# Scan stage of a hybrid kernel: skip term on TensorE, normalising on ScalarE, end-decay product on GpSimd

## What is computed

```python
xn = (x - mean) * rsqrt(var + 1e-5) * ln_w + ln_b          # over channels
z, xBC, dt = split(in_proj_w @ xn)                         # 256, 256 + 32 + 32, 8 rows
xBC = silu(depthwise_conv_3x3(xBC) + conv_b)               # xs (8 heads x 32), B, C
dt = softplus(dt + dt_bias);  A = -exp(A_log)
# chunks of 128 positions, 8 an image
Acs = cumsum(dt * A)                                        # within the chunk
Y_diag = sum_s C_q.B_s * exp(Acs_q - Acs_s) * (xs*dt)_s     # s <= q, by head
state  = sum_q B_q * exp(Acs_end - Acs_q) * (xs*dt)_q       # end decay
Y_off  = C_q . previous_state * exp(Acs_q)
y = Y_diag + Y_off + D * xs                                 # skip term D*xs
y = y * silu(z);  y = y * rsqrt(mean(y*y) + 1e-5) * rms_w
x = x + out_proj_w @ y
```

## Time and profile before

| what | value |
|---|---|
| median of 3 runs | 2489.66 us (2485.59 to 2492.06) |
| profiled execution, its own time | 2490.13 us |
| span of the profile | 2488.4 us, 41622 instructions |
| PE busy | 2235.4 us (90%) |
| DVE busy | 1699.6 us (68%) |
| ACT busy | 1279.2 us (51%) |
| POOL busy | 1635.1 us (66%) |
| mean granted TensorE clock | 0.914 |

### The profile page before, as it was taken

One profiled execution on the slowest core, in us unless ns is written; L12 is line 12 of the kernel. 1 busy time (PEld: TensorE's weight loads), 2 busy tenths in 40 slices (PEclk: granted clock), 3 DMA queues, 4 the chain that ended last, 5 costly groups with the idle time before them and its releaser, 6 DMA issues. The chain is left out here.

```text
span 2488.4 us, 41622 instructions
## 1 busy us (share of the span) xinstructions
PE 2235.4 (90%) x12035; PEld 1803.0 (72%) x12035; DVE 1699.6 (68%) x4560; ACT 1279.2 (51%) x2815; POOL 1635.1 (66%) x1774
## 2 busy tenths in 40 slices
PE   4798898899886999999999999999999997499994
PEld 2466666666664888888888888888888886388883
DVE  5787987888745667767767777677777775244444
ACT  3454554554532666666666666666666664133331
POOL 2688878887861666576685776766757766355551
PEclk9887887787876999999999999999999998699996
DMA  2930000000000001010010010100100100355555
GB/s 89 387 128 9 9 9 1 9 1 1 18 5 23 1 2 24 2 30 13 7 36 1 12 31 4 37 4 8 35 2 12 31 4 30 129 194 189 197 180 203
DMA packets 135413, 131.05 MB, mean 53 GB/s; under 512 B 82885, under 2 KB 101359, under 8 KB 135190
## 3 DMA queue, kind: packets, MB, share of 16 engines
q1 hardware_dynamic: 124950, 107.12, 14.1%
q0 software_dynamic: 9088, 17.07, 2.0%
q10 hardware_dynamic: 1152, 4.19, 0.4%
HBM read 64.78 MB, written 65.10 MB: 52 GB/s over the span
## 5 line engine op out<-in xcount | busy, mean ns | idle before, releaser
L1191 POOL TENSOR_TENSOR plo<-pf,phi 128x512 fp32r<-128x512 f32 (+3 forms) x768 | 775.3, 1018 | 414.5 <-ACT phi L1414 385.3
L1412 ACT ACTIVATE pf<-psum 128x512 f32<-128x512 f32 (+3 forms) x768 | 379.3, 494 | 479.1 <-PE psum L1252 339.1
L1414 ACT ACTIVATE phi<-psum 128x512 fp32r<-128x512 f32 (+3 forms) x768 | 377.1, 491 | 0.0
L1301 PE MATMUL psum<-xT,qT 128*128 128x512 f32 (+3 forms) x768 | 286.1, 372 | 43.9 <-DVE nmax L1557 30.2
L1557 DVE CUSTOM_DVE_ANT_0 masked<-psum,ahead_wide 128x128 f32<-128x128 f32 (+3 forms) x512 | 248.2, 485 | 66.9 <-PE psum L1301 60.2
L1250 PE MATMUL psum<-phi,x_tok 128*128 128x512 f32 (+3 forms) x768 | 289.0, 376 | 0.8 <-POOL plo L1191 0.8
L1252 PE MATMUL psum<-qT,xT 128*128 128x512 f32 (+3 forms) x768 | 266.5, 347 | 0.0
L1251 PE MATMUL psum<-qT,xT 128*128 128x512 f32 (+3 forms) x768 | 266.1, 347 | 0.0
L1250 PE MATMUL psum<-qT,xT 128*128 128x512 f32 (+3 forms) x768 | 265.7, 346 | 0.0
L1251 PE MATMUL psum<-plo,x_tok 128*128 128x512 f32 (+3 forms) x768 | 265.0, 345 | 0.0
L1252 PE MATMUL psum<-phi,x_tok 128*128 128x512 f32 (+3 forms) x768 | 265.0, 345 | 0.0
(11 more groups left out here) (288 smaller groups left out, 5324.5 us busy)
## 6 DMA issues: line engine op xcount, KB each, us to landing
wg<-turned_w SPq DMA_DIRECT2D x39, 874.0 KB
routed<-empty SPq DMA_DIRECT2D x1, 34056.0 KB, 95.7
xg<-routed SPq DMA_DIRECT2D x39, 264.0 KB
qT<-nmax SPq DMA_DIRECT2D x512, 0.5 KB
y<-chosen SPq DMA_DIRECT2D x8, 1024.0 KB, 10.3
turned_w<-wT SPq DMA_DIRECT2D x8, 874.0 KB
x_in_sb<-in_x SPq DMA_DIRECT2D x8, 512.0 KB, 3.3
out<-o_st ACTq DMA_DIRECT2D x8, 512.0 KB, 5.2
```

The lines of the kernel that those rows point to most:

```text
L1191: g_.tensor_tensor(plo[:, T % RP, 0:n], pf[:, T % RP, 0:n], phi[:, T % RP, 0:n].bitcast(F32), ALU.subtract).then_inc(a["low_ready"], 1)
L1301: t.matmul(bank[3][:, 0:n], qT[:, g % 2, 0, i * P:(i + 1) * P], xT[:, b % 2, 0, k0:k0 + n], start=True, stop=True).then_inc(a["peak_ready" ...
L1412: s_.activation(pf[:, T % RP, 0:n], bank[T % RS][:, 0:n], ACT.Exp)
L1414: s_.activation(phi[:, T % RP, 0:n], bank[T % RS][:, 0:n], ACT.Exp).then_inc(a["high_ready"], 1)
```

## The change

Three operations of the scan change engines, and one becomes part of another.

1. The skip term: `dx` and its add on GpSimd go. At the setup VectorE makes `skip_w`, two 128x128 matrices with D on the diagonal. In TensorE's `chunk_y`, ahead of each four heads, xs of the chunk times `skip_w` starts the sum in the half bank, and the heads add to it.
2. The normalising goes from VectorE to ScalarE: `rstd * x + shift`, with `shift` = -mean * rstd made by GpSimd in `deviation` in two more small operations. ScalarE does all eight at j = 6, behind the exponentials and ahead of the first `turned_back`.
3. `Xd` goes from VectorE to GpSimd, a step later, in a new function `chunk_end`; VectorE copies the last column of Ldec (128x8) to `to_end` for it, and waits for `tok_ready` instead of `tok_copied` and `xdt_ready`.

Waits that stood on `tok_ready` for xs no longer being read now stand on `y_ready`, since TensorE reads xs a step later.

```diff
 GpSimd, deviation(n)
                         g_.tensor_tensor(rstd[:, :], mvx[:, :, 1], epst[:, 0:1].to_broadcast([P, NC]), ALU.add).then_inc(s["vx_ready"], 1)
-                        pool.wait_ge(s["vx_ready"], n + 1)
+                        g_.tensor_tensor(shift[:, :], mvx[:, :, 0], minus[:, 0:1].to_broadcast([P, NC]), ALU.mult).then_inc(s["vx_ready"], 1)
+                        pool.wait_ge(s["vx_ready"], 2 * (n + 1))
                         g_.tensor_tensor(rstd[:, :], rstd[:, :], mhalf[:, 0:1].to_broadcast([P, NC]), ALU.pow
                                          ).then_inc(s["rstd_ready"], 1)
+                        pool.wait_ge(s["rstd_ready"], n + 1)
+                        g_.tensor_tensor(shift[:, :], shift[:, :], rstd[:, :], ALU.mult).then_inc(s["shift_ready"], 1)
 GpSimd, silu_x(n, m)
-                        need(pool, "tok_ready", (n - 1) * NC)
+                        need(pool, "y_ready", (n - 1) * NC)
 GpSimd, end of chunk_in(g), and a new function
-                        need(pool, "yd_ready", g - 3)
-                        g_.tensor_tensor(dx[:, g % 4, :].rearrange("p (h d) -> p h d", d=HD), xs3,
-                                         dvec[:, :].unsqueeze(2).to_broadcast([P, NH, HD]), ALU.mult).then_inc(s["dx_ready"], 1)
+                    def chunk_end(g):
+                        pool.wait_ge(s["to_end_ready"], g + 1)
+                        pool.wait_ge(s["xdt_ready"], g + 1)
+                        need(pool, "st_ready", g - 1)
+                        g_.tensor_tensor(Xd[:, g % 2, :].rearrange("p (h d) -> p h d", d=HD),
+                                         xdt[:, g % 2, :].rearrange("p (h d) -> p h d", d=HD),
+                                         to_end[:, g % 4, :].unsqueeze(2).to_broadcast([P, NH, HD]), ALU.mult).then_inc(s["xd_ready"], 1)
 GpSimd, chunk_gate(g)
-                        pool.wait_ge(s["dx_ready"], g + 1)
-                        g_.tensor_tensor(y1[:, g % 4, :], y1[:, g % 4, :], dx[:, g % 4, :], ALU.add).then_inc(s["yd_ready"], 1)
-                        pool.wait_ge(s["yd_ready"], g + 1)
 GpSimd, the loop, between chunk_rs(step - 3) and chunk_in(step)
+                        if 0 <= step - 1 < G:
+                            chunk_end(step - 1)
 TensorE, chunk_y(g)
                         for h in range(NH):
+                            if h % 4 == 0:
+                                m = h // 4
+                                t.matmul(bank[4][:, DI + m * P:DI + (m + 1) * P], xsC[:, n % 2, m, sl], skip_w[:, m, :], start=True, stop=False)
                             last = t.matmul(bank[4][:, DI + h * HD:DI + (h + 1) * HD], Ldec[:, g % 2, h, :],
-                                            xdt[:, g % 2, h * HD:(h + 1) * HD], start=True, stop=True)
+                                            xdt[:, g % 2, h * HD:(h + 1) * HD], start=False, stop=(h % 4 == 3))
 ScalarE, new, both halves called at j == 6 ahead of turned_back(nn, 0)
+                    def normalise(n, hf):
+                        act.wait_ge(s["shift_ready"], n + 1)
+                        need(act, "tb_ready", 2 * (n - 1) + hf + 1)
+                        for c in range(4 * hf, 4 * hf + 4):
+                            last = a_.activation(xt[:, c, :], t_all[:, n * NC + c, :], ACT.Identity, scale=rstd[:, c:c + 1],
+                                                 bias=shift[:, c:c + 1])
+                        last.then_inc(s["xt_ready"], 1)
 VectorE, setup
+                    for m in range(2):
+                        link(v.tensor_tensor(skip_w[:, m, :].rearrange("p (h d) -> p h d", d=HD), ident[:, :].rearrange("p (h d) -> p h d", d=HD),
+                                             dvec[:, 4 * m:4 * m + 4].unsqueeze(2).to_broadcast([P, 4, HD]), ALU.mult))
 VectorE, normalise(n, hf) and its two calls at j == 6 are taken out
 VectorE, chunk_in(g)
                         dve.wait_ge(s["decay_ready"], g + 1)
-                        dve.wait_ge(s["tok_copied"], g + 1)
-                        dve.wait_ge(s["xdt_ready"], g + 1)
-                        need(dve, "st_ready", g - 1)
-                        v.tensor_tensor(Xd[:, g % 2, :].rearrange("p (h d) -> p h d", d=HD),
-                                        xdt[:, g % 2, :].rearrange("p (h d) -> p h d", d=HD),
-                                        Ldec[:, g % 2, :, P - 1:P].to_broadcast([P, NH, HD]), ALU.mult).then_inc(s["xd_ready"], 1)
-                        dve.wait_ge(s["xd_ready"], g + 1)
+                        dve.wait_ge(s["tok_ready"], g + 1)
+                        need(dve, "xd_ready", g - 3)
+                        v.tensor_copy(to_end[:, g % 4, :], Ldec[:, g % 2, :, P - 1]).then_inc(s["to_end_ready"], 1)
+                        dve.wait_ge(s["to_end_ready"], g + 1)
 SP, the wait ahead of the two attention weights
-                    sp.wait_ge(s["tok_ready"], (B - 1) * NC)
+                    sp.wait_ge(s["y_ready"], (B - 1) * NC)
```

More of the change, by code:

```diff
@@ L163, in hybrid_kernel @@
             xdt = sb1("xdt", [P, 2, DI])
-            dx = sb1("dx", [P, 4, DI])
+            skip_w = sb1("skip_w", [P, 2, P])
+            to_end = sb1("to_end", [P, 4, NH])
+            shift = sb1("shift", [P, NC])
+            minus = sb1("minus", [P, 1])
             Xd = sb1("Xd", [P, 2, DI])
@@ L184, in hybrid_kernel @@
                 conv_done tap_scaled tap_added th_made th_ready xs_ready thc_made thc_ready bcs_ready bc_ready resid_T resid_ready
-                tok_ready tok_copied seg_ready decay_ready gl_ready xd_ready xdt_ready dx_ready st_ready state_ready y_ready y_drained
-                yd_ready yg_ready ssq_ready ms_ready rs_ready b6_ready yT_copied t_ready t_drained mv_ready ve_ready rs2_ready lnx_ready
+                tok_ready tok_copied seg_ready decay_ready gl_ready xd_ready xdt_ready st_ready state_ready y_ready y_drained
+                to_end_ready shift_ready yg_ready ssq_ready ms_ready rs_ready b6_ready yT_copied t_ready t_drained mv_ready ve_ready rs2_ready lnx_ready
                 xnT_copied dve_step pool_step pad_zero s_faded edec_ready sums_apart chooser""".split()
@@ L248, in _ @@
                     g_.memset(ones_col[:, :], 1.0).then_inc(s["pool_step"], 1)
+                    g_.memset(minus[:, :], -1.0).then_inc(s["pool_step"], 1)
                     g_.memset(epst[:, :], EPS).then_inc(s["pool_step"], 1)
-                    pool.wait_ge(s["pool_step"], 8)
+                    pool.wait_ge(s["pool_step"], 9)
                     for m in (ident, ident_bf):
@@ L676, in chunk_in @@
                         need(act, "st_ready", g - 3)
-                        need(act, "dx_ready", g - 3)
                         need(act, "xdt_ready", g - 3)
@@ L731, in _ @@
                             if j == 6:
+                                normalise(nn, 0)
+                                normalise(nn, 1)
                                 turned_back(nn, 0)
@@ L804, in statistics @@
                         dve.wait_ge(s["resid_ready"], 2 * n + hf + 1)
-                        need(dve, "vx_ready", n)
+                        need(dve, "vx_ready", 2 * n)
                         for c in range(4 * hf, 4 * hf + 4):
@@ L813, in statistics @@
                         last.then_inc(s["mvx_ready"], 1)
[L815 to L822, removed]
                     def step_sizes(n):
@@ L950, in _ @@
                                 cumulated(n)
-                        if has(nn) and j == 6:
-                            normalise(nn, 0)
-                            normalise(nn, 1)
                         if has(n):
```

## The result

The changed kernel takes 2458.69 us (median; 2450.2 to 2465.33), the kernel before 2487.62 in the same comparison: ratio 0.9884, interval [0.9845, 0.9922], so 1.2% or 29 us faster. Forecast was 2497, with 2478 as the low end. The profiled execution took 2450.2 us, span 2448.5; it is the fastest of the four, so the traces differ by 40 us where the medians differ by 29. Its scan ends at 702 us instead of 744, and what follows is as long as before, within 2 us.

What follows compares the result with a forecast made beforehand. No engine alone bounded the scan; the path passed between TensorE, VectorE and GpSimd. Terms came to +10.9 us before the clock, +7.1 with its -3.8, so 2490.1 + 7.1 = 2497 us; range 2478 to 2511.

Steps and rivals of the forecast that it cites:

- Clock, -3.8: TensorE's clock in the scan: shorter waits before steps 3, 5 and 6 give one more short image, -3.8 us.
- rival A: TensorE's clock in the scan: four more images take the short form, 2482 us, 2474 with taps at their bound; chance 0.25.
- Lighter GpSimd, -1.5: VectorE's taps in the scan: less GpSimd port time makes them faster, -1.5 us, bounds 0 and minus 10.
- steps 3 to 6, six images: Skip product in step 3 costs 0.5 us an image; Xd off VectorE gains in steps 4 and 5; sum -11.1.
- step 6 to the next image's 2, six images: Longer wait before the first turning back, +1.2 us an image; skip products +2.6; Xd's gain in step 2 -0.6; sum +19.2.
- seventh image: Seventh image of the scan: a larger gain from Xd off VectorE than in the others, -1.9 us in all.
- last image: Last image, where TensorE sets the pace: eight chunks at 0.53 us and the last at 1.0, +5.2 us.
- lead-in: Before the scan overlaps: slower normalising on ScalarE, the shift, making skip_w, and 0.2 for the second image, +1.8 us.
- steps 7, where I feared 2.4: VectorE's 128x8 copy could take Xd's 2.4 us beside GpSimd, some 10 us over the scan; left out of the sum.
- my three signs of being wrong: Low clock's share changes; 128x8 copy over 0.5 us in the median; GpSimd's Xd is what the state product waits for.
- rival B: Step 6's longer wait keeps TensorE's clock low through steps 7 and 0, 2.5 us an image: 2516 us; chance 0.17.
- Rivals C and D: Scan, both 2490 us: freed ports speed VectorE's taps (C); VectorE's bound hides part of the skip cost (D); together 0.16.

Runs made afterwards that it cites:

- e4: Kernel before plus two TensorE products a chunk whose result is overwritten, nothing taken off any engine: 2479.2 us, ratio to before 0.9967.
- e6: Changed kernel without the skip term's two TensorE products a chunk, so D*xs is left out of the result: 2485.4 us, ratio to before 0.9997.
- e5: Kernel before without the skip term: dx and its add off GpSimd, no products added: 2452.2 us, ratio to before 0.9866.
- e1: Kernel before with only the skip term moved to TensorE, dx and its add off GpSimd: 2459.7 us, ratio to before 0.9878.
- e3: Kernel before with only Xd moved to GpSimd, and the 128x8 copy on VectorE: 2488.6 us, ratio to before 1.0019.
- e7: Changed kernel with the normalising back on VectorE, so only skip term and Xd moved: 2442.8 us, ratio to before 0.9836.
- e8: Changed kernel with Xd back on VectorE, so only skip term and normalising moved: 2512.2 us, ratio to before 1.0088.
- e2: Kernel before with only the normalising moved to ScalarE, shift on GpSimd: 2501.1 us, ratio to before 1.0077.
- e11: e8 plus eight useless TensorE products an image ahead of its step 6 wait for the normalised image: 2465.7 us, ratio to before 0.9916.
- e13: Kernel before plus six useless TensorE products an image ahead of its step 6 wait for the normalised image: 2474.4 us, ratio to before 0.9941.

## Why the prediction was wrong

**The steps that failed** are two terms of the sum, both of the right sign and far too small.

*Clock, -3.8.* "I take one more short image." All images became shorter than the short one (78.4 against 83.5). I had counted what TensorE's added products cost and treated the clock as luck. It went from 0.79 to 0.90 in the scan, and TensorE was busy 29 us less for 34 us more of work. e4 shows that the same products on the kernel before pay for themselves and bring 8 us, e6 that without them the changed kernel loses 27, not all of it by the clock alone. My rival A was the right mechanism with too low a price: at its bound it gave 2474.

*Lighter GpSimd, -1.5.* This term priced the taps alone, and they did not get faster at all (median 1585 ns against 1586 in the earlier trace rows). But e5 measured the relief at 36 us, and e1 shows that with the products in its place it is the whole gain. What did get shorter was Xd on VectorE and the waits on xdt, which my sum had only as a gain of Xd's move, and the stretch from step 6 to 7. Xd's move brings nothing on the kernel before (e3).

*Where the sum was off.* Added up from VectorE's decay products of the two traces (us, after less before; the terms of the taps, the drain and the clock had no place there and are left out):

| stretch | in the sum | measured |
|---|---|---|
| steps 3 to 6, six images | -11.1 | -32.4 |
| step 6 to the next image's 2, six images | +19.2 | -3.9 |
| steps 2 to 3, six images | 0 | -3.1 |
| seventh image | -1.9 | -7.9 |
| last image | +5.2 | +7.4 |
| lead-in | +1.8 | +2.1 |

In the first row the path was as I drew it. TensorE's wait of 1.79 before step 6 went, and 1.3 of it reached the path of step 5 to 6. The other 2.0 us of the 3.3 (11.2 to 7.9) I had not: step 6's turning and exponents took 1.9 us at full clock instead of 3.0, mostly at half, and in step 5 the full level came back sooner. The clock from step 5 to 6 rose from 0.68 to 1.00. e1 and e5, with GpSimd lighter and nothing else off VectorE, keep 10.8 us there, and e6, e7 and e8, each with one of the parts missing, take 9.6 or more, so this place needs all three. In the second row the products' cost and the longer wait are there, and the clock makes up for them: 0.64 to 0.80 from step 6 to 7, 0.67 to 1.00 from step 0 to 1.

**What held.** The skip term's products take 0.63 us a chunk from start to start at full clock (two halves of 0.32) and 1.2 at half, against 0.53 and 1.0; with the heads behind them they add 0.45 and 0.86 to what the heads alone took. ScalarE's normalising takes 0.49 each, against 0.45, and the wait before the first turning back 2.79, against 2.7 (in the kernel before it was 6.9 us over the six images, 1.15 each and not my row's 1.46); that this part costs time is shown (e2), 0.8% alone. The first decay product comes at 92.3 us instead of 90.2, against 1.8.

The 128x8 copy takes 0.17 in the median, against 0.21. The Trainium skill, page "SBUF — State Buffer", section "Who interferes with whom", says that a VectorE copy in a 2-port mode and GpSimd lock each other out of the port pair that they share. The trace agrees with up to 1.77 us, in the first image's step 3 beside GpSimd's sum of taps. In steps 7, where I feared 2.4, it took 0.17, and 0.78 once. Over the 64 these come to 8.7 us above the median, 0.2 to 0.4 each in most images' steps 4 to 6; how much of that is path no run shows.

The wait ahead of step 6's turning is gone, the one ahead of step 5's is not (2.11), and the one ahead of step 3's fell from 3.30 to 0.85, more than the 1 that I had said. Of my three signs of being wrong one came, the changed clock; the copy stayed under 0.5 us, and the state product waits for Xd only twice. Two slips in my working change nothing: rival B in half of the images gives 2508, not 2509, and the chances add up to 0.37 within 0.3% and 0.38 slower.

**Rival B** is not this kernel but e8: there the clock does stay low from the 2.79 us wait on, through step 7, at 6.7 us an image (against e11), where I had given it 2.5. The changed kernel has the same wait and escapes in five of the six images. In its first it does not, and TensorE's clock there is

```profile
144.00:160.00 16.00, 16.00 (x61) 11.40 (x61) 4.55 (x9) 8.70 (x18) 9.41 (x14) 0.57 0.19 71
```

The Trainium skill says in "TensorE: Matmul & The Clock Gate", section "What's actually happening", that activity releases the throttle; e4, e11 and e13 agree, with 8, 46 and 15 us for added activity.

**Rivals C and D** fell: the taps are no faster, and the scan's time moved by 41 us in the traces.

## What to carry to other kernels

When the granted clock of a stretch is well below 1, price a change by both levels, and test the clock first: useless products in a wait of the engine cost one run, and a gain by them is the clock's. At 0.78 in the kernel before they gained 15 us, at 0.81 in e8 46, and at 0.83 in e5 and 0.91 in e7 nothing. Added TensorE work is not a cost in such a stretch until an experiment says so, and the parts of a change are not worth the same alone and in company (Xd on GpSimd: 0, 17 or 53 us). Here the best version leaves the normalising on VectorE: e7, 2442.8 us, 1.6% faster than before and 16 us faster than the change.

## What the runs showed of the hardware that I had not expected

The same 2.79 us wait of TensorE was followed by some 4 us at the lower level in five images of the changed kernel and by 13 us in e8; the work behind the wait was nearly the same. In e11, 0.96 us of wait behind 1.91 us of useless products was not followed by the lower level at all. Which of these comes is much of what spreads the kernels with the skip term on TensorE over 70 us (2443 to 2512). From step 6 to 7, added up over the first six images, e7 and e8 differ by 57 us, and within each of the two ways to normalise the time mostly goes with the clock of that stretch (us, clock):

| normalising on | kernels |
|---|---|
| VectorE | before 72.9, 0.64; e3 65.2, 0.75; e4 58.7, 0.78; e5 49.4, 0.86; e7 46.2, 0.92; e1 46.4, 1.00 |
| ScalarE | e8 102.8, 0.60; e2 84.2, 0.64; e6 85.1, 0.70; changed 75.6, 0.80; e11 62.4, 0.99 |

That the clock is the cause is shown by added work alone for e8 (e11) and the kernel before (e13, 43.0 at 0.96); for the others it is argued. Why the changed kernel escapes and e8 does not was not tried. In e8 TensorE had also waited 1.48 us ahead of step 6's turning and ran at half clock from there, and in the changed kernel it had not. But in the changed kernel's first image it had run for 6.3 us without a wait, at full clock, and the low level still held for 12 us behind the 2.79.
